# A graph network in four layers: the edge network's second product computed feature by edge, and turned back by PE in layer 2

## The reference

```
L0: mean over the edges (and the node itself) of (h @ W)[src], + b
L1: lap = sum over edges of h[src] * w;  leaky_relu((h + lap) @ W1 + (h * lap) @ W2 + b1 + b2), normalised
L2: hn = h @ Wn.T + bn
    ef = ssp(e @ We1.T + be1);  ef = ssp(ef @ We2.T + be2)        # 100000 x 128, ssp(x) = softplus(x) - log 2
    agg = sum over edges of hn[src] * ef;  fc2(ssp(fc1(agg)))
L3: attention with 4 heads over the same edges, layer norm, relu
```

## Time and profile before

| | |
|---|---|
| three runs | 5386.12 us median (5382.66 to 5396.66) |
| the profiled execution | 5406.18 us, its span 5404.9 us |
| PE, matmuls | busy 2637.8 us (49%), 13386 instructions |
| PE, weight loads | busy 2190.4 us (41%) |
| DVE | busy 2598.9 us (48%) |
| ACT | busy 1829.3 us (34%) |
| POOL | busy 3092.4 us (57%), of it 2960.4 us in 3136 gathers |
| granted TensorE clock | 0.70 of full speed |

### The profile page before, as it was taken

The page is one execution under the profiler, slowest core; times in us unless marked ns, Lnnn a source line. Parts: engine busy times, 40 slices in busy tenths (PEclk is TensorE's granted clock), DMA queues, the critical chain, the costliest instruction groups (busy, mean ns, idle before and its releaser), DMA issues.

```text
span 5404.9 us, 58867 instructions
## 1 busy us (share of the span) xinstructions
PE 2637.8 (49%) x13386; PEld 2190.4 (41%) x13386; DVE 2598.9 (48%) x7117; ACT 1829.3 (34%) x4243; POOL 3092.4 (57%) x3262
## 2 busy tenths in 40 slices
PE   2544545435355555544433233333645655555667
PEld 1444444433344444443333232222434444444446
DVE  3333333325355455444533233332457777777778
ACT  2333333302133233320411111111545555555555
POOL 3566666663565566665566666666355555555553
PEclk8777777766677767766766666666867777777668
DMA  4333333321233333321222222223181111111110
GB/s 112 92 99 99 97 99 100 96 50 42 73 98 89 94 96 98 89 76 36 79 85 87 85 86 86 87 85 90 54 138 41 39 40 40 41 40 40 41 40 25
DMA packets 226598, 403.92 MB, mean 75 GB/s; under 512 B 59386, under 2 KB 124879, under 8 KB 226256
## 3 DMA queue, kind: packets, MB, share of 16 engines
q0 software_dynamic: 100608, 208.65, 16.0%
q10 hardware_dynamic: 52816, 115.13, 7.1%
q1 hardware_dynamic: 72840, 76.37, 4.6%
HBM read 332.15 MB, written 67.78 MB: 74 GB/s over the span
## 4 chain that ended last, share of the span: by engine, by line
another core or an unknown queue 16%; DVE 15%; issue 10%; PE 4%; DVEq 3%; ACT 2%; ACTq 0%; POOL 0%; DMA 0%; SPq 0%
DVE t_acc L1352 5%; DVEq L654 3%; PE ps L749 2%; DVE t_acc L788 2%; DVE t_hT L1252 2%; DVE t_hT L1301 1%; DVE t_hT L1291 1%; DVE t_hT L1297 1%; DVE t_hT L1287 1%; DVE t_hT L1304 0%; DVE t_acc L800 0%; ACT t_acc L1067 0%; ACT t_hT L1315 0%; DVE t_hT L1284 0%
## 5 line engine op out<-in xcount | busy, mean ns | idle before, releaser
L679 POOL DMA_INDIRECT t_work<-d_T,t_tabG x3136 | 2960.4, 944 | 2077.7 <-SPq L717 1022.5
L800 DVE TENSOR_TENSOR t_acc<-t_acc,ps 128x128 f32 (+1 forms) x732 | 207.7, 284 | 1755.1 <-remote 1460.4
L585 PE MATMUL ps<-t_wts,t_acc 128*128 128x128 f32 x1568 | 332.1, 397 | 574.4 <-DVE t_acc L631 490.4
L749 PE MATMUL ps<-t_work 128*128 x2608 | 431.3, 324 | 262.2 <-issue 110.7
L585 PEld LDWEIGHTS ps<-t_wts,t_acc 128*128 128x128 f32 x1568 | 308.1, 301 | 591.7 <-issue 591.7
L749 PEld LDWEIGHTS ps<-t_work 128*128 128x128 f32 x2608 | 409.9, 238 | 323.4 <-issue 322.7
L749 PE MATMUL ps<-t_acc,t_work 128*128 128x128 f32 x1304 | 260.6, 371 | 562.9 <-DVE t_acc L788 305.5
L609 ACT ACTIVATE t_acc<-ps,t_bcol 128x1024 f32<-128x1024 f32 x98 | 109.1, 1113 | 1239.9 <-DVE ps L623 979.1
L1342 PE MATMUL ps<-t_work,t_hT 128*128 x1960 | 413.2, 375 | 181.0 <-ACT t_hT L1330 81.2
L831 ACT COPY ps<-t_acc 128x512 f32 x244 | 142.0, 589 | 1051.9 <-issue 427.6
L749 PEld LDWEIGHTS ps<-t_acc,t_work 128*128 128x128 f32 x1304 | 235.2, 274 | 585.4 <-DVE t_acc L788 317.6
(11 more groups left out here) (169 smaller groups left out, 4622.1 us busy)
## 6 DMA issues: line engine op xcount, KB each, us to landing
t_work<-d_T,t_tabG POOLq DMA_INDIRECT x3136
d_edge_net<-t_acc ACTq DMA_DIRECT2D x98, 512.0 KB
t_acc<-d_edge_net SPq DMA_DIRECT2D x98, 512.0 KB
t_acc<-in_edge_attrT ACTq DMA_DIRECT2D x96, 512.0 KB
t_acc<-d_T ACTq DMA_DIRECT2D x12, 790.1 KB
d_T<-t_acc SPq DMA_DIRECT2D x20, 256.0 KB, 2.3
t_acc<-d_T SPq DMA_DIRECT2D x4, 790.1 KB
d_T<-t_acc SPq DMA_DIRECT2D x10, 266.0 KB, 3.2
```

The lines of the kernel that those rows point to most:

```text
L585: last = pe.matmul(ps[:, 6 + k // QUAD, k % QUAD * D:(k % QUAD + 1) * D], sp1[:, k * P:(k + 1) * P], WE2, start=True, stop=True)
L679: pool.indirect_dma_start(out=work[:, at:at + width], out_offset=None, in_=table, in_offset=bass.IndirectOffsetOnAxis(ap=idx[:, g * QUAD + ...
L749: last = pe.matmul(sums(layer, s, width), masks[s % MASKS][:, k, :], rows_k, start=(k == 0), stop=(k == QUAD - 1))
L800: dve.tensor_tensor(out=o, in0=o, in1=sums(layer, s, width), op=ALU.add).then_inc(e_acc[layer], 1)
```

## The change

The second product of the edge network becomes like the first: We2 stands and the first layer's result moves in 512 columns, which gives feature by edge. Its bias then belongs to the partition and goes into the column operands that ACT's chain and DVE's maximum take anyway; DVE's addition and its semaphore go. Three of the five places in the hand-written order are moved or dropped. What is stored and loaded is feature by edge, so in layer 2 ACT copies a group to one of three SBUF buffers (`brought`), PE turns it with four transposes into the PSUM bank (`turn_net`), and DVE multiplies as before. PE's queue holds the turn of step t + 3 ahead of the sum of step t. PE no longer loads its control numbers in layer 2, since it needs none there.

```diff
-        bias = sb("bias", [P, 6, D])
-        bcol = sb("bcol", [P, 8])
+        bias = sb("bias", [P, 5, D])
+        bcol = sb("bcol", [P, 11])
...
 net_second(n):
-            for k in range(2 * QUAD):
-                last = pe.matmul(ps[:, 6 + k // QUAD, k % QUAD * D:(k % QUAD + 1) * D], sp1[:, k * P:(k + 1) * P], WE2,
-                                 start=True, stop=True)
+            for h in range(2):
+                last = pe.matmul(ps[:, 6 + h, :], WE2, sp1[:, h * GRP:(h + 1) * GRP], start=True, stop=True)
             last.then_inc(s_zb, 1)
 chain_second(n):
-            act.wait_ge(s_bb, n + 1)
+            act.wait_ge(s_zb, n + 1)
...
-            for j, (dst, src, f, bb, sc) in enumerate(softplus_part(z_b, forty, v, v, v)):
+            for j, (dst, src, f, bb, sc) in enumerate(softplus_part(z_b, down_e2, v, v, v)):
-        def net_bias(n):
-
-            dve.wait_ge(s_zb, n + 1)
-            z = ps[:, 6:8, :].rearrange("p h (k d) -> p (h k) d", d=D)
-            dve.tensor_tensor(out=z, in0=z, in1=BE2.unsqueeze(1).to_broadcast([P, 2 * QUAD, D]), op=ALU.add)\
-                .then_inc(s_bb, 1)
 soft_second(n):
-            dve.scalar_tensor_tensor(out=halved(efo[n % 2]), in0=z_b, scalar=-LOG2, in1=halved(soft_b), op0=ALU.add,
+            dve.scalar_tensor_tensor(out=halved(efo[n % 2]), in0=z_b, scalar=less_e2, in1=halved(soft_b), op0=ALU.add,
                                      op1=ALU.max).then_inc(s_pb2, 1)
...
+        brought = [acc[:, SQ + k * GRP:SQ + (k + 1) * GRP] for k in range(MASKS)]
...
-        FIRST_AT, SOFT_A_AT, SECOND_AT, BIAS_AT, SOFT_B_AT = 2, 6, 9, 11, 13
+        FIRST_AT, SOFT_A_AT, SECOND_AT, SOFT_B_AT = 2, 6, 8, 12
...
+            def turn_net(s):
+
+                pe.wait_ge(e_br, s + 1)
+                if s >= BANKS:
+                    pe.wait_ge(e_mul, s - BANKS + 1)
+                for k in range(QUAD):
+                    last = pe.transpose(beside_rows[s % BANKS][:, k * P:(k + 1) * P],
+                                        brought[s % MASKS][:, k * P:(k + 1) * P], ident)
+                last.then_inc(e_cp, 1)
+
+            if layer == 2:
+                for s in range(BANKS - 1):
+                    turn_net(s)
+                for t in range(STEPS):
+                    if t + BANKS - 1 < STEPS:
+                        turn_net(t + BANKS - 1)
+                    sum_step(t, None)
+                return
...
 bring_net():
-                if s >= BANKS:
-                    act.wait_ge(e_mul, s - BANKS + 1)
-                act.copy(beside_rows[s % BANKS], ef_ring[:, bass.ds(slot, GRP)]).then_inc(e_cp, 1)
+                if s >= MASKS:
+                    act.wait_ge(e_cp, s - MASKS + 1)
+                act.copy(brought[s % MASKS], ef_ring[:, bass.ds(slot, GRP)]).then_inc(e_br, 1)
```

More of the change, by code:

```diff
@@ L227, in build @@
             ld_w.add(act.dma_start(wts[:, k, :], a[name]))
-        for k, name in enumerate(("b0", "b1a", "b1b", "bn", "bf2", "be2")):
+        for k, name in enumerate(("b0", "b1a", "b1b", "bn", "bf2")):
             ld_w.add(act.dma_start(bias[:, k, :], a[name].to_broadcast([P, D])))
-        B0, B1, B1B, BN, BF2, BE2 = (bias[:, k, :] for k in range(6))
-        ld_w.add(act.dma_start(bcol[:, 0:1], a["be1"]))
-        ld_w.add(act.dma_start(bcol[:, 1:2], a["bf1"]))
+        B0, B1, B1B, BN, BF2 = (bias[:, k, :] for k in range(5))
+        for k, name in enumerate(("be1", "bf1", "be2")):
+            ld_w.add(act.dma_start(bcol[:, k:k + 1], a[name]))
         eps_c = small[:, 49:50]
@@ L537, in build @@
         need(dve, ld_w.mark)
-        V.did(dve.tensor_scalar(bcol[:, 2:4], bcol[:, 0:2], -1.0, 40.0, ALU.mult, ALU.add))
-        V.did(dve.tensor_scalar(bcol[:, 4:6], bcol[:, 0:2], -LOG2, None, ALU.add))
+        V.did(dve.tensor_scalar(bcol[:, 3:6], bcol[:, 0:3], -1.0, 40.0, ALU.mult, ALU.add))
+        V.did(dve.tensor_scalar(bcol[:, 6:9], bcol[:, 0:3], -LOG2, None, ALU.add))
         V.did(dve.tensor_tensor(out=B1, in0=B1, in1=B1B, op=ALU.add))
-        V.did(dve.memset(bcol[:, 6:7], 40.0))
-        prepared = V.did(dve.memset(bcol[:, 7:8], 0.5))
-        forty, halfc = bcol[:, 6:7], bcol[:, 7:8]
+        V.did(dve.memset(bcol[:, 9:10], 40.0))
+        prepared = V.did(dve.memset(bcol[:, 10:11], 0.5))
+        forty, halfc = bcol[:, 9:10], bcol[:, 10:11]
+        down_e1, down_f1, down_e2 = (bcol[:, k:k + 1] for k in range(3, 6))
+        less_e1, less_f1, less_e2 = (bcol[:, k:k + 1] for k in range(6, 9))
         need(act, prepared)
@@ L594, in chain_first @@
             v = halved(soft_a)
[L595 removed]
+            for j, (dst, src, f, bb, sc) in enumerate(softplus_part(z_a, down_e1, v, v, v)):
                 if j:
@@ L732, in sum_groups, with sum_step @@
         def sum_groups(layer, width):
-            def step(s):
-                edge, _, _, slot = control(ENG.PE, s)
+            def sum_step(s, slot):
                 if layer == 2:
                     pe.wait_ge(e_mul, s + 1)
-                else:
-                    pe.wait_ge(e_rdy[layer], edge)
                 pe.wait_ge(e_msk[layer], s + 1)
-                if s >= len(SUMS[layer]):
-                    pe.wait_ge(e_acc[layer], s - len(SUMS[layer]) + 1)
+                if s >= 2 and len(SUMS[layer]) == 2:
+                    pe.wait_ge(e_acc[layer], s - 1)
                 for k in range(QUAD):
@@ L751, in step @@
                 last.then_inc(e_mm[layer], 1)
+            def turn_net(s):
[14 more added lines that the diff above has]
+                return
             first = HALFNET * layer
             for t in range(STEPS):
-                step(t)
-                if layer == 2:
-                    continue
+                edge, _, _, slot = control(ENG.PE, t)
+                pe.wait_ge(e_rdy[layer], edge)
+                sum_step(t, slot)
                 if due(t, FIRST_AT) is not None:
@@ L869, in edge_loop @@
             if layer == 2:
-                over += [(e_mul, STEPS), (e_cp, STEPS)]
+                over += [(e_mul, STEPS), (e_br, STEPS), (e_cp, STEPS)]
             return over
@@ L1061, in soft @@
             need(act, z1[g])
-            for j, (dst, src, f, bb, sc) in enumerate(softplus_part(z, bcol[:, 3:4], ar, ae, al)):
+            for j, (dst, src, f, bb, sc) in enumerate(softplus_part(z, down_f1, ar, ae, al)):
                 if j:
@@ L1070, in soft @@
                 need(dve, added[g - 2])
-            f1[g] = V.did(dve.scalar_tensor_tensor(out=spn[g % 2][:, 0:w], in0=z, scalar=bcol[:, 5:6],
+            f1[g] = V.did(dve.scalar_tensor_tensor(out=spn[g % 2][:, 0:w], in0=z, scalar=less_f1,
                                                    in1=al[:, 0:w], op0=ALU.add, op1=ALU.max))
```

11 lines of the change are left out of this document (4 added, 7 removed).

## The result

The changed kernel is slower. Five runs of each give a median of 5439.92 us (5429.97 to 5446.95) against 5396.66 us (5382.66 to 5403.25), ratio 1.0082, 95% interval 1.006 to 1.0105. The forecast was 5366 us, faster; the time lies at the very end of the range (5295 to 5440 us). The profiled execution took 5433.48 us (span 5432.1), 27.3 us more than that of before.

The account below looks back on a forecast made before the run. POOL's gathers, held by waits for ring space that late PE reports end, were taken to bound layers 0 to 2. Terms -27 - 3 - 10 + 20 = -20 us gave 5386.2 us profiled, 5366 against the median; range 5295 to 5440 us.

Parts of the forecast that it names:

- What bounds the kernel: Layers 0 to 2: POOL's gathers set the pace, slowed by waits for ring space that late PE reports end; 639 us winnable.
- Layers 0 and 1, DVE: -27 us: Bias addition gone, second maximum slightly slower: 113.3 us less DVE work, priced at 0.24; bounds 0 and -113 us.
- under the 25 us: Sign of being wrong: layers 0 and 1 together less than 25 us quicker.
- an exchange rate: Price of DVE work in gather time, 0.24 us lost per us, read from layer 1 against layer 0.
- Layers 0 and 1, PE: -3 us: Second product in fewer, wider instructions: 0 to -70 us of PE, at 0.09 giving 0 to -6 us.
- Order: -10 us: Layers 0 and 1: second product issued a step earlier; most of line 616's wait only takes another name; bounds 0 and -100.
- Rival C: Order in layers 0 and 1 is worth most: line 616's wait really goes, -61 us for -10, 5315 us; chance 0.15.
- Layer 2: +20 us: Four PE turns in each of 244 steps, 220 us of PE priced at 0.09; upper bound +220 us.
- rival A: Turns stand in layer 2's path: one step of three pays in full, 73 us for 20, 5419 us; chance 0.27.
- the four cases: Forecast 5366 us (0.38); turns in path 5419 (0.27); nothing measurable about 5386 (0.20); order worth most 5315 (0.15).
- PE's new wait for the copy: 0: Layer 2: PE waits for the copy of step s + 3 ahead of sum s; counted 0, group mostly there.
- ACT's copy to SBUF: 0: Layer 2: ACT's copy writes SBUF instead of PSUM, 588 against 589 ns, so no cost.

Follow-up runs that it names:

- e6: Kernel before with only the first 32 gathers of each of layers 0 to 2 made; 3621.57 us in a late session, kernel before 5340.85 us.
- e7: Changed kernel with only the first 32 gathers of each of layers 0 to 2 made; 3573.79 us in a late session.
- e11: Kernel before with layer 2 alone as in the changed one, late session; 5357.69 against 5327.41 us, ratio 1.0053.
- e3: Changed kernel with the sum of step t ahead of the turn of step t + 3 in PE's queue; 4540.07 us, ratio 1.0009 to the kernel before.
- e10: Kernel before with four PE turns more per step of layer 2, read by nobody and waiting only for the sum's bank; ratio 1.0003.
- e12: Kernel before with four unread PE turns more per step of layer 2, run again; ratio 1.0004, prompt session.
- e13: Kernel before with four unread PE turns more per step of layer 2, run again; ratio 1.0001, prompt session.
- e15: Kernel before with four unread PE turns more per step of layer 2, run again; ratio 0.9999, prompt session.
- e17: Kernel before with four unread PE turns more per step of layer 2, run again; ratio 0.9998, prompt session.
- e18: Kernel before with four unread PE turns more per step of layer 2, run again; ratio 1.0, prompt session.
- e16: Changed kernel with eight buffers in place of three for ACT's copy in layer 2; ratio 1.0007 to the kernel before, prompt session.
- e5: Changed kernel itself, unchanged, in a prompt session; 4541.19 against 4534.69 us for the kernel before, ratio 1.0008.
- e9: Changed kernel with layer 2 as before, without turning; ratio 1.0001 to the kernel before, prompt session.
- e4: Kernel before without DVE's bias addition, ACT's second chain waiting for PE instead; 4534.8 us, ratio 0.9999, prompt session.
- e1: Changed kernel with layer 2 as before, without turning; 4536.44 against 4535.89 us for the kernel before, ratio 1.0002, prompt session.
- e14: Changed kernel with layer 2 as before, run again; ratio 1.0002 to the kernel before, prompt session.
- e2: Kernel before with layer 2 alone as in the changed one; 4539.99 us, ratio 1.0006, prompt session.
- e8: Kernel before with layer 2 alone as in the changed one, run again; ratio 1.0003, prompt session.

## Why the prediction was wrong, point by point

*What bounds the kernel.* Right for the sessions of the comparison: POOL waits for ring space, and a late report of PE ends the wait. That this is a condition of a session and not of the kernel, the trace of one session could not show. That nobody works meanwhile was too much said: PE's own instructions come slowly then, as the last section shows.

*Layers 0 and 1, DVE: -27 us.* This is the term that failed, with the order below: in the profiles both layers gave -15 us together where -40 stood, under the 25 us that the prediction had named as a sign of being wrong. No run separates the DVE term from the order and PE's term in a late session, so what each gave by itself stays open. The step behind it was to price work by an exchange rate, 0.24 us lost per us of DVE, read from the difference of two layers. Those layers differ by a multiply that stands in every step between mask and sum, while the bias addition stood in one step of four, in the stretch between two waits for PE. Taking it away let DVE arrive earlier at the next wait: 56 of 57 us in layer 0 and 40 of 57 in layer 1 are found again as idle time. e6 and e7, without gathers, won 47 us in layer 0 and 2 in layer 1 by the same edit. One rate for both layers cannot give either pair. The term's bounds, 0 and -113 us, held.

*Layers 0 and 1, PE: -3 us.* The second product took 280.8 us of busy time where I had line 576's 262.1; the mean of an instruction was 857 ns, line 576's had been 803. With 280.8 for 332.1 us the busy time fell by 51 us, within the 0 to 70 that stood there, and no effect of its own is visible.

*Order: -10 us.* The direction was right and stronger than said: the whole of line 616's 416.2 us is gone (0.6 left), and the add's idle time grew by 212 us in layer 0 and 300 in layer 1. Rival C, which paid for this wait with 5315 us, is refuted. The wait moved on to the next instruction for the same releaser, as the prediction had said of most of it; 0, its own bound, is nearer to what the rows show than -10, though no run has the order by itself. The add had waited 54 and 66 us for PE's own end, and now 232 and 205.

*Layer 2: +20 us, measured +33 in the profiles and +28 (20 to 36) in e11.* Size and sign about right, but by luck: the rate had no mechanism behind it. The mechanism in the rows is rival A's: the sum behind the turns ends too late to be reported before the gathers hold the reports up, and the fifth add of a run falls out of it (23 of 33 runs had five before, none of 40 after). A priced it at 73 us (one step of three pays in full). POOL's waits grew by 43 us and six stops over the layer; against it the sums got quicker (351 ns a matmul for 371, clock 0.63 for 0.60). A as a forecast, 5419 us, was the nearest of the four cases, but not for the right reasons: it had layers 0 and 1 at their full -40.

*PE's new wait for the copy: 0.* Held in the late sessions: 7.1 us in the window, 23.7 over the layer. In the prompt ones it was 380.9 us, for which nothing was lost because POOL set the pace. The multiply hardly waited for the turn's report either (0.0 us in the window, 5.2 over the layer). ACT waits 600.8 us for "remote". By the code it waits for SP's word, which has a name of its own in the row, and for the report of the turn three steps back; before the change it waited for DVE's multiply. Nobody waits for ACT for long. This is why I hold the turn's report for harmless and its place ahead of the sum for the cause. It is read from the traces of the comparison and of e11; the runs that would have shown it by the time (e3 for the order, e10, e12, e13, e15, e17 and e18 for the turns alone, e16 for the report) all fell into prompt sessions. So what in layer 2's half costs its 28 us is argued from rows and not shown by an experiment.

*ACT's copy to SBUF: 0.* Wrong by 28 ns each: 617 ns for SBUF to SBUF, 589 to PSUM, 7 us of ACT beside other work. The row that I compared with had PSUM as its source. The Trainium skill's "ScalarE: Activation LUTs", What happens when an exp ACTIVATE runs, Step-by-step, has ScalarE quicker towards PSUM; with the same source this trace agrees.

*Sum.* Forecast -40 + 20 = -20 in the profile (25 us too much in layers 0 and 1, 13 too little in layer 2); measured -15 + 33 + 5 (layer 3) + 4 (between) = +27. The rest to the medians' +43 is where the two executions lie: I had taken the one before as 20 us above its median, over five runs it was 9.5, and the changed one's lay 6.4 below. Whether layers 0 and 1 win anything in the medians stays open: 0.82% in all less 0.53% for layer 2 alone leaves +0.29% for them, an estimate across two sessions whose interval (about 0.0 to 0.6%) nearly reaches zero, against -15 us in the one pair of profiles. The -40 us are in neither.

## What to carry to other kernels

Before pricing work taken from an engine, find the next thing for which that engine will wait; if it is the same releaser as now, most of the work comes back as waiting (here 56 and 40 of 57 us). A rate read from the difference between two stages did not carry over here to work at another place of the step. And where a producer's report has to arrive inside a short opening, count the time from the start of the opening: here 1 us of turns ahead of the sum went with one add less in most runs.

## What the runs showed of the hardware

*Reports of PE that come late.* With the same kernel and the same chip number the time was 4536 us in one session and 5327 in another. In late sessions, PE's completion reaches DVE late while POOL issues gathers without a pause: 5.89 us in the round above, and the add at 3328.97 us takes a sum that ended at 3311.70 by its record, 17.3 us earlier, only after POOL has stopped. DVE's add waited 1645.7 us for such "remote" causes over the changed kernel's span, and in the prompt session (e5) 1625.0 of its 1633.7 us of waiting ended with PE's own end. With the gathers taken away in a late session (e6, e7) DVE's adds had no such wait in the three windows. Why a session is one or the other is open.

In that condition PE's own instructions come slowly too, late in a run of gathers. One row for each matmul of four turns in the changed kernel, start us first:

```profile
3323.18 0.37 PE L751 MATMUL ps<-t_cst,t_acc 128*128 128x128 f32 x1 [2.43 <-issue]
...
3324.61 0.37 PE L751 MATMUL ps<-t_cst,t_acc 128*128 128x128 f32 x1 [1.05 <-issue]
...
3326.01 0.37 PE L751 MATMUL ps<-t_cst,t_acc 128*128 128x128 f32 x1 [1.03 <-issue]
```

1.4 us apart, where they need 0.26 each. Gaps over 0.9 us make up 174.0 of the 197.1 us of "issue" ahead of line 751; in the prompt session that line waits for ACT's copy alone (380.9 of 381.3 us).

*Turns and the clock.* In one prompt session the same stretch of layer 2 ran without turns (e9) at a granted clock of 0.55 and with the turns alone (e10) at 0.70. The windows of all engines, e9 and e10, us, then PE, PEld, DVE, ACT, POOL busy:

```profile
2250.00:3100.00 850.00, 401.35 (x1696) 355.29 (x1696) 324.71 (x636) 122.40 (x213) 642.77 (x680) 0.55 0.35 105
```

```profile
2250.00:3100.00 850.00, 484.31 (x2547) 435.70 (x2546) 325.46 (x639) 122.48 (x213) 642.46 (x682) 0.70 0.36 106
```

The sums' matmuls of two thirds of the steps took 418 ns each in e9 and 376 in e10. So turns beside sums do lift the clock here, from mostly 1.2 GHz towards 2.4. The other prompt traces agree: 0.54 and 0.55 without turns (e4, e1, e14), 0.71 to 0.73 with them (e2, e3, e5, e8, e12, e13, e15 to e18). The Trainium skill says in "TensorE: Matmul & The Clock Gate", Part 4: PE-mode transpose, that the full clock doesn't engage for turns; the measurement decides, for turns between products. Turns with no product beside them no run has. In the comparison the clock of layer 2 rose too, from 0.60 to 0.63.
